# A transformer decoder layer on Trainium2: residuals added by TensorE, LayerNorm sums formed by ScalarE

## Chip, cores and metric

The kernel runs on 1 core of one Trainium2 chip. The metric is the device time of one execution in microseconds (us), the median of 3 runs.

## What is computed

Batch 8, sequence 512, width 512, 16 heads of 32. Three blocks, each followed by a residual sum and a LayerNorm for the first two, and once more for the MLP:

```python
x1 = layernorm(x  + self_attention(x))                 # rope, softmax over 512 keys, no output projection
x2 = layernorm(x1 + tree_attention(x1, ctx) @ Wo.T + bo)
y  = layernorm(x2 + relu(x2 @ w1 + b1) @ w2 + b2)      # width 2048
```

`tree_attention` builds keys and values from `ctx`, adds a binary tree of sums above them (1023 nodes), and lets every position attend to itself and to 12 nodes that an index table names.

## The kernel before

All large products are made in fp16 in three parts: an fp32 operand is split into `hi` and `lo`, and `hi*hi + hi*lo + lo*hi` is accumulated in fp32. Engines run their own instruction streams and meet only through semaphores; the order on each engine is written out by hand.

The first stage walks over the batch. `iteration` has 32 steps `d` (a head pair and a quarter of the keys each): scores and row maxima (`rows_ps`, `neg_max`, VectorE), exponentials (`e_ps` to `probsT`, ScalarE) and values (`o_ps`) with a lag of 12 to 14 steps, and beside them the projections of the next batch (`AUX_AT`), the tree (`tree`, GpSimd) and the splitting of later weights. LayerNorm of the batch before lies in steps 15 to 19 (`LN_STEPS`): `add_residual` on GpSimd, `norm_stats` and `norm_apply` on VectorE, `rstd_of` on GpSimd. At step 19 SyncE (SP) stores the four tiles of x1 in fp32 to `x1_dram` (L365), from which the second stage reads them. A last `iteration(..., tail=True)` finishes the last batch; then all engines meet at the border of the stages.

The second stage works on tiles of 128 positions (4 per batch, 32 in all); two tiles are a round. VectorE and GpSimd do tree attention for round r+1 while TensorE and ScalarE do the MLP of round r.
- VectorE, `attention`, per tile: `key_sums` for the groups 2 to 5 of gathered rows and the own row (L1358, L1362, L1367), `shift` (L1385 to L1391), `x2_sum` of the tile before (L1451 residual, L1454 and L1457 statistics), `key_sums` for groups 0 and 1 of the next tile, `normalise` (L1397 to L1404), `values` (L1416, L1420, L1426; accumulated in PSUM tile `O`). In each second tile `y_sums` (L1466, L1469) for the round before lies behind the first accumulation.
- GpSimd, `attention`, per tile: `x2_rstd_of`, the value products of groups 3, 4 and 5 (`weight_values`), 12 gathers of 128 rows of 4 KB (L1533), each after the slot that it fills was accumulated, then `y_adds` (L1595) or `y_rstds`. There are 8 slots for groups of two gathers.
- TensorE and ScalarE, `mlp`, per round: 16 chunks `c` of 128 hidden columns. TensorE: `hidden(c)` (12 products), then the attention products that are due, then `mlp_out(c-1)` (6 products), then `hidden_minus_hi(c)`. ScalarE: `hid_hi(c)` (L1288), its attention work, `hid_lo(c)` (L1311). `OUT_AT`, `QUERY_AT`, `EXP_AT`, `APPLY_AT`, `X2_AT` say at which chunk the attention work of the two tiles lies: `copy_o` (L1248) and the output projection, the query projection, the exponentials (L1252), the x2 normalisation (L1259), the x2 transpose.
- A transposed tile is split in turns: TensorE transposes into `TURN`, ScalarE copies `hi` (L1233), TensorE subtracts it (`turn_minus_hi`), ScalarE copies `lo` (L1235).
- `PROJ` and `O` are one PSUM bank. `copy_acc` copies the MLP's result at the start of the next round (L1274), `y_apply` normalises it at the end of that round (L1266).

Middle rounds run in hardware loops of two rounds (one loop pass is four tiles).

## Time and profile before

| | |
|---|---|
| runs (us) | 2434.88, 2438.08, 2434.06; median 2434.88 |
| profiled execution | 2434.74 us, its span 2432.9 us |
| TensorE busy | 2066.2 us (85%) |
| VectorE busy | 1701.0 us (70%) |
| GpSimd busy | 1050.4 us (43%) |
| ScalarE busy | 985.0 us (40%) |
| granted TensorE clock, mean | 0.937 |

The span runs from the first to the last instruction. In the rows, DVE is VectorE, ACT is ScalarE, POOL is GpSimd, PE is TensorE, SPq is the queue of SyncE that issues DMAs. A timeline row is start (us), duration (us), engine, line, operation, output<-input, shape, count, and in brackets the idle time before it and what ended that. A group row has the count, then busy us, mean ns of one, then idle us before them. Matmuls are pipelined, and their ends are modelled.

### The profile page before, as it was taken

Reading aid. Unit: us, or ns where it says so; the run is one execution under the profiler, and the core shown is the slowest. Engines: PE = TensorE matmul, PEld = TensorE weight load, DVE = VectorE, ACT = ScalarE, POOL = GpSimd, SP = SyncE. Lnnn points to the kernel's source line nnn. Section 1 sums busy time; section 2 is a strip of 40 time slices with the busy share of each in tenths; the row PEclk is TensorE's granted clock in tenths of the full one; section 3 lists DMA queues with packets and bytes.
Section 4 is the critical chain, followed back from the end, with each engine's and each line's share of the span. In section 5 each row is a group of like instructions: output and inputs, shape, how many; then the busy total and the mean of one; then the engine's idle time right before and its main releaser. Section 6 shows DMA issues by size and latency. Waiting matters only on the chain.

```text
span 2432.9 us, 33921 instructions
## 1 busy us (share of the span) xinstructions
PE 2066.2 (85%) x10944; PEld 1014.4 (42%) x10944; DVE 1701.0 (70%) x2289; ACT 985.0 (40%) x1579; POOL 1050.4 (43%) x1132
## 2 busy tenths in 40 slices
PE   5899999999999999994239888898888898888987
PEld 2333333333333333331015554455554555545554
DVE  8565647475565647552788888898888988988950
ACT  3355445454545455553013333333333333333333
POOL 3232334242433424233354655655656546556521
PEclk9999999999999999997669999999999999999999
DMA  6442424343343424233945656556556556566510
GB/s 206 133 135 91 131 84 147 106 139 118 118 148 117 139 76 145 88 126 119 361 165 202 229 173 222 202 189 227 191 202 232 180 201 225 185 220 215 177 63 27
DMA packets 189290, 392.50 MB, mean 161 GB/s; under 512 B 20948, under 2 KB 82516, under 8 KB 189144
## 3 DMA queue, kind: packets, MB, share of 16 engines
q1 hardware_dynamic: 133848, 189.44, 24.4%
q0 software_dynamic: 55296, 201.35, 23.6%
q8 instruction: 63, 1.03, 0.2%
q14 instruction: 83, 0.68, 0.1%
HBM read 312.86 MB, written 77.59 MB: 160 GB/s over the span
## 4 chain that ended last, share of the span: by engine, by line
DVE 25%; issue 11%; DMA 8%; PE 5%; POOL 3%; SPq 1%; DVEq 0%; ACT 0%; POOLq 0%
DVE bank L1420 8%; DMA nb<-kv_flat,idx_rows 7%; DVE logits L1367 4%; DVE nb L1416 4%; POOL nb L1533 2%; PE bank L1136 2%; DVE nb L1358 2%; PE bank L1117 2%; DMA own<-kv_flat 1%; DVE stats L1454 1%; DVE x L1451 1%; DVE own L1362 1%; DVE bank L1426 1%; DVE stats L1466 1%; PE bank L1084 1%
## 5 line engine op out<-in xcount | busy, mean ns | idle before, releaser
L697 DVE TENSOR_REDUCE neg_max<-rows_ps 128x2 f32<-128x1024 f32 x256 | 312.5, 1221 | 309.0 <-PE rows_ps L492 308.1
L1533 POOL DMA_INDIRECT nb<-kv_flat,idx_rows x384 | 367.6, 957 | 136.0 <-issue 85.0
L1358 DVE TENSOR_TENSOR nb<-nb,bank 128x1024 f32<-128x1024 f32 x192 | 230.6, 1218 | 137.1 <-DMA nb<-kv_flat,idx_rows 108.6
L617 ACT ACTIVATE probsT<-e_ps 128x1024 f32<-128x1024 f32 x256 | 262.0, 1023 | 158.4 <-PE e_ps L520 158.1
L1117 PE MATMUL bank<-x2T_hi,w_hi_sb 128*128 128x256 f16 x1024 | 285.9, 279 | 5.6 <-issue 4.8
L1117 PE MATMUL bank<-x2T_lo,w_hi_sb 128*128 128x256 f16 x1024 | 285.2, 279 | 0.0
L1117 PE MATMUL bank<-x2T_hi,w_lo_sb 128*128 128x256 f16 x1024 | 284.5, 278 | 0.0
L510 PE MATMUL o_ps<-probsT,v_sb 128*33 128x512 f32 x1024 | 272.9, 612 | 6.3 <-ACT oT L614 6.1
L1420 DVE TENSOR_TENSOR bank<-bank,nb 128x512 f32<-128x512 f32 x384 | 268.1, 698 | 13.7
L1561 POOL TENSOR_TENSOR nb<-nb,weights 128x1024 f32<-128x1024 f32 x96 | 182.7, 1917 | 155.6 <-DVE weights L1404 154.9
L1367 DVE TENSOR_REDUCE logits<-nb 128x32 f32<-128x1024 f32 x192 | 229.9, 1211 | 0.0
L443 PE MATMUL aux<-in_hi,w_hi 128*128 128x512 f16 x512 | 196.8, 384 | 38.0 <-DVE w_lo L653 28.1
L1136 PE MATMUL bank<-w_hi_sb,hid_hi 128*128 128x512 f16 x512 | 203.9, 398 | 19.9 <-ACT hid_lo L1311 19.9
L1136 PE MATMUL bank<-w_hi_sb,hid_lo 128*128 128x512 f16 x512 | 204.9, 400 | 0.0
L1136 PE MATMUL bank<-w_lo_sb,hid_hi 128*128 128x512 f16 x512 | 204.8, 400 | 0.0
L765 POOL TENSOR_TENSOR lo<-rot,hi 128x512 f16<-128x512 f32 x64 | 78.0, 1219 | 290.8 <-DVE hi L676 290.8
L1311 ACT ACTIVATE hid_lo<-bank,b_sb 128x256 f16<-128x256 f32 x256 | 120.5, 471 | 194.0 <-PE bank L1124 194.0
L443 PE MATMUL aux<-in_hi,w_lo 128*128 128x512 f16 x512 | 196.7, 384 | 0.0
L443 PE MATMUL aux<-in_lo,w_hi 128*128 128x512 f16 x512 | 196.6, 384 | 0.0
L492 PE MATMUL rows_ps<-k_stack,q_stack 96*128 96x512 f16 x512 | 153.8, 381 | 37.6 <-DVE neg_max L697 37.4
L1288 ACT ACTIVATE hid_hi<-bank,b_down 128x256 f16<-128x256 f32 x256 | 121.1, 473 | 155.0 <-PE bank L1117 154.1
L760 POOL TENSOR_TENSOR in_lo<-in_sb,in_hi 128x2048 f16<-128x2048 f32 x16 | 68.7, 4295 | 226.1 <-ACT in_hi L554 226.1
(147 smaller groups left out, 3583.2 us busy)
## 6 DMA issues: line engine op xcount, KB each, us to landing
kv_flat<-kv_nat SPq DMA_DIRECT2D x128, 256.0 KB, 3.4
own<-kv_flat SPq DMA_DIRECT2D x32, 512.0 KB
q_stack<-qk_dram SPq DMA_DIRECT2D x96, 128.0 KB, 2.9
k_stack<-qk_dram SPq DMA_DIRECT2D x96, 128.0 KB, 3.2
piece<-in_pieces SPq DMA_DIRECT2D x40, 256.0 KB, 3.0
in_sb<-in_xT SPq DMA_DIRECT2D x8, 1024.0 KB, 6.5
in_sb<-in_ctxT SPq DMA_DIRECT2D x8, 1024.0 KB, 5.8
qk_dram<-hi SPq DMA_DIRECT2D x32, 256.0 KB, 2.2
```

The lines of the kernel that those rows point to most:

```text
L443: mm = pe.matmul(o[:], w_part[:, w, c, f], x_part[:, which, c, :], start=c + k == 0, stop=c == KC - 1 and k == 2)
L492: mm = pe.matmul(rows_ps[:, i, :], q_stack[0:M_ROW, h, qt * P:(qt + 1) * P], k_stack[0:M_ROW, h, :], start=True, stop=True)
L510: mm = pe.matmul(O[side * SIDE:side * SIDE + VW, :], v_sb[:, slot, kt, 2 * pair + side, :], probsT[:, (d - V_LAG) % TT, side, :], start=kt ...
L617: act.activation(probsT[:, (d - E_LAG) % TT, :, :], e_ps[:], ACT.Exp, scale=1.0 / (Q_UP * K_UP))\
L697: dve.tensor_reduce(neg_max[:, g % 2, at:at + 2], rows_ps[:], AX.X, ALU.max, negate=True).then_inc(max_done, 1)
L1117: mm = pe.matmul(HB[c % 2][:, 0:RW], w[:, k, c * P:(c + 1) * P], x_part[:, k, half * RW:(half + 1) * RW], start=k + i == 0, stop=k == KC - ...
L1136: mm = pe.matmul(ACC[i][:], h_part[:, c % 2, i * P:(i + 1) * P], w[:, c, :], start=False, stop=c == WC - 1 and k == 2)
L1358: dve.tensor_tensor(kk, kk, q.unsqueeze(1).to_broadcast([P, GN, D]), ALU.mult)\
L1367: dve.tensor_reduce(logits[:, lt % 2, g * GN:(g + 1) * GN, :], nb[:, slot(lt, g), :, 0:D].rearrange("p n (h d) -> p n h d", h=H), AX.X, AL ...
L1420: dve.tensor_tensor(O[:], O[:], nb[:, slot(lt, g), k, D:2 * D], ALU.add).then_inc(o_part, 1)
L1533: pool.indirect_dma_start(nb[:, slot(lt, g), k, :], None, kv_flat, bass.IndirectOffsetOnAxis(idx_rows[:, lt, at:at + 1], 0))\
L1561: pool.tensor_tensor(vv, vv, w, ALU.mult).then_inc(v_mul_pool, 1)
```

## The change

In the first stage, x1 is split after LayerNorm: ScalarE copies each tile to fp16 (`x1_parts` hi), GpSimd subtracts (lo); this lies in steps 18, 19 and 22, the stores of two tiles each in steps 20 and 24, and the tail has 25 steps in place of 20. The query's rope tables are those of the key, and the query's scale is put into the copy from PSUM.

In the second stage x1 comes in as two fp16 parts. The query needs no split: 8 fp16 transposes into one bank and one copy. `project_out` adds x1 by two products with `plus_up` (64 times the identity), `mlp_out(0)` adds x2 by 8 products of 128 columns for each tile. ScalarE copies PROJ and ACC with an accumulated sum (`x2_sum`, `copy_acc`), then forms the sum of squares about the mean with `Square` (`x2_square`, `y_square`). VectorE's `x2_sum` and `y_sums` and GpSimd's `y_adds` are gone. `x2_rstd_of` moves from the head of the next tile's GpSimd work to the end of the tile's own. `OUT_AT`, `EXP_AT` and the first `QUERY_AT` and second one move by one chunk; `y_apply` moves to chunk 7 of the round.

```diff
-TAIL = 20
+TAIL = 25
-X1_STORE, X_ROWS_LOAD, X_ROWS_BIAS = 19, 21, 27
+X1_SPLIT = {18: (0,), 19: (1,), 22: (2, 3)}
+X1_STORE, X_ROWS_LOAD, X_ROWS_BIAS = (20, 24), 24, 27
-OUT_AT, QUERY_AT, EXP_AT, APPLY_AT, X2_AT = (1, 9), (2, 8), (4, 12), (5, 13), (6, 14)
+OUT_AT, QUERY_AT, EXP_AT, X2_AT = (2, 10), (3, 9), (5, 13), (6, 14)
+SUM_AT, SQUARE_AT, APPLY_AT = (3, 11), (4, 12), (5, 13)
+Y_SQUARE_AT, Y_APPLY_AT = 1, 7
...
# first stage: load_x waits for the split, not the store; two stores
-                    sp.wait_ge(x1_stored, START + b * (16 * TT))
+                    sp.wait_ge(x1_lo_done, START + b * TT)
+                def store_x1(b, k):
+                    sp.wait_ge(x1_lo_done, START + b * TT + 2 * k + 2)
...
# first stage, ScalarE
+                            for t in X1_SPLIT.get(d, ()):
+                                act.wait_ge(x1_ready, START + (b - 1) * TT + t + 1)
+                                act.wait_ge(x1_stored, START + (b - 1) * 32 + 16 * (t // 2))
+                                act.activation(x1_parts[:, t % 2, 0, :], xb[:, t, :], ACT.Copy).then_inc(x1_hi_done, 1)
# first stage, GpSimd
+                            for t in X1_SPLIT.get(d, ()):
+                                pool.wait_ge(x1_hi_done, START + (b - 1) * TT + t + 1)
+                                pool.tensor_tensor(x1_parts[:, t % 2, 1, :], xb[:, t, :], x1_parts[:, t % 2, 0, :],
+                                                   ALU.subtract).then_inc(x1_lo_done, 1)
...
# second stage, SyncE
                 def load_res(b, lt):
-                    sp.wait_ge(out_added, START + b * TT + lt)
+                    sp.wait_ge(proj_ready, START + b * TT + lt)
# second stage, TensorE
                 def turn_query(b, lt):
-                    turn(turn_of(b, lt, "q"), x1_in[:, lt % 2, :])
+                    pe.wait_ge(turn_copied, START + turn_of(b, lt, "q"))
+                    for k in range(2):
+                        for f in range(KC):
+                            at = (k * KC + f) * P
+                            mm = pe.transpose(TURN16[:, at:at + P], x1_in[:, lt % 2, k, f * P:(f + 1) * P], plus_one[:])
+                    mm.then_inc(turn_ready, 1)
                 def project_out(b, lt):
-                    pe.wait_ge(out_added, START + b * TT + lt)
+                    pe.wait_ge(res_loaded, START + (b * TT + lt) * 16 + 16)
+                    for k in range(2):
+                        pe.matmul(PROJ[:], plus_up[:], x1_res[:, k, :], start=False, stop=False)
# mlp_out, c == 0
+                            for k in range(KC):
+                                for x_part in (x2T_hi, x2T_lo):
+                                    pe.matmul(ACC[i][:, k * P:(k + 1) * P], x_part[:, k, rows], plus_up[:],
+                                              start=False, stop=False)
...
# second stage, ScalarE
+                def turned_query(b, lt):
+                    act.wait_ge(turn_ready, START + turn_of(b, lt, "q") + 1)
+                    act.activation(actT[:, ACT_SLOT["q", lt % RT]].rearrange("p k c t -> p (k c t)"), TURN16, ACT.Copy)\
+                        .then_inc(turn_copied, 1)
+                def x2_sum(b, lt):
+                    act.wait_ge(proj_ready, START + n + 1)
+                    act.activation(x2[:, s, :], PROJ[:], ACT.Copy, scale=1.0 / W_UP, accum_out=sums[:, s:s + 1])\
+                        .then_inc(x2_summed, 1)
+                    act.wait_ge(x2_summed, START + n + 1)
+                    act.activation(neg_mean[:, s:s + 1], sums[:, s:s + 1], ACT.Copy, scale=-1.0 / D)\
+                        .then_inc(x2_centre, 1)
+                def x2_square(b, lt):
+                    act.wait_ge(x2_centre, START + n + 1)
+                    act.wait_ge(x2_squared, START + n)
+                    act.activation(squares[:, 0, :], x2[:, s, :], ACT.Square, bias=neg_mean[:, s:s + 1],
+                                   accum_out=sum_squares[:, s:s + 1]).then_inc(x2_squared, 1)
# copy_acc: the same accum_out; y_square(b, half) squares both tiles of a round at chunk 1
...
# second stage, VectorE
-                    dve.scalar_tensor_tensor(out=x2[:, lt, :], in0=PROJ[:], scalar=1.0 / W_UP, in1=x1_res[:],
-                                             op0=ALU.mult, op1=ALU.add).then_inc(out_added, 1)
-                    dve.bn_stats(stats[:, s, :], x2[:, lt, :]).then_inc(x2_part, 1)
-                    dve.bn_aggr(mean_var[:, s, :], stats[:, s, :]).then_inc(x2_stats, 1)
-                        dve.bn_stats(stats[:, s, :], y_sb[:, lt, :]).then_inc(y_part, 1)
-                        dve.bn_aggr(mean_var[:, s, :], stats[:, s, :]).then_inc(y_stats, 1)
# values
-                        dve.wait_ge(o_copied, START + n)
+                        dve.wait_ge(x2_summed, START + n)
# second stage, GpSimd, attention
-                        if not (early and lt == 0):
-                            x2_rstd_of(*last_tile(b, lt))
...
-                            y_adds(b - 1, half_)
-                        if lt % RT == 1 and not early:
                             y_rstds(b - 1, half_)
+                        x2_rstd_of(b, lt)
```

## Rows read from the trace of the kernel before

**Rows 1.** Busy time by stage: us, then PE, PEld, DVE, ACT, POOL, clock, DMA share, GB/s

```profile
60.00:1050.00 990.00, 932.17 (x4365) 362.69 (x4364) 586.63 (x826) 490.49 (x643) 340.32 (x351) 0.99 0.39 120
...
1300.00:2347.00 1047.00, 904.53 (x5456) 544.22 (x5454) 904.23 (x1188) 377.87 (x760) 582.51 (x641) 0.93 0.58 201
```

**Rows 2.** Timeline of VectorE: the weights of tiles 4 and 30

```profile
1337.25 0.37 DVE L1404 TENSOR_TENSOR weights<-weights,total 128x208 f32<-128x208 f32 x1
...
2301.15 0.37 DVE L1404 TENSOR_TENSOR weights<-weights,total 128x208 f32<-128x208 f32 x1
```

**Rows 3.** Timeline of VectorE over one tile, from weights to weights

```profile
1782.95 0.37 DVE L1404 TENSOR_TENSOR weights<-weights,total 128x208 f32<-128x208 f32 x1
...
1805.93 1.22 DVE L1358 TENSOR_TENSOR nb<-nb,bank 128x1024 f32<-128x1024 f32 x1 [0.95 <-DMA nb<-kv_flat,idx_rows]
...
1811.86 0.69 DVE L1451 SCALAR_TENSOR_TENSOR x<-bank,x_res 128x512 f32<-128x512 f32 x1
...
1813.61 2.35 DVE L1358 TENSOR_TENSOR nb<-nb,bank 128x1024 f32<-128x1024 f32 x2
...
1818.14 0.50 DVE L1397 TENSOR_REDUCE total<-weights 128x16 f32<-128x208 f32 x1
...
1819.25 0.37 DVE L1404 TENSOR_TENSOR weights<-weights,total 128x208 f32<-128x208 f32 x1
```

**Rows 4.** Timeline of GpSimd in that tile: first and eighth gather

```profile
1788.34 1.05 POOL L1533 DMA_INDIRECT nb<-kv_flat,idx_rows  x1 [1.06 <-DVE bank L1420]
...
1799.02 0.94 POOL L1533 DMA_INDIRECT nb<-kv_flat,idx_rows  x1 [0.30 <-issue]
```

**Rows 5.** Timeline of VectorE in the next tile, the last of a loop pass

```profile
1823.73 0.68 DVE L1466 BATCH_NORM_STATS2 stats<-y_sb 128x6 f32<-128x512 f32 x1
...
1825.62 0.70 DVE L1420 TENSOR_TENSOR bank<-bank,nb 128x512 f32<-128x512 f32 x1
...
1838.88 2.35 DVE L1358 TENSOR_TENSOR nb<-nb,bank 128x1024 f32<-128x1024 f32 x2 [4.96 <-issue]
...
1857.92 0.37 DVE L1404 TENSOR_TENSOR weights<-weights,total 128x208 f32<-128x208 f32 x1
```

**Rows 6.** Timeline of ScalarE in these tiles

```profile
1795.88 0.60 ACT L1248 ACTIVATE o_sb<-bank 128x512 f32<-128x512 f32 x1 [6.42 <-DVE bank L1420]
...
1815.34 0.37 ACT L1252 ACTIVATE weights<-logits 128x208 f32<-128x208 f32 x1
...
1850.58 0.38 ACT L1252 ACTIVATE weights<-logits 128x208 f32<-128x208 f32 x1 [1.75 <-DVE logits L1391]
```

**Rows 7.** Busy time after two waits for `copy_o`, columns as in rows 1

```profile
1685.00:1691.00 6.00, 5.41 (x33) 3.19 (x34) 1.34 (x2) 2.94 (x6) 4.71 (x5) 1.00 0.99 353
1796.00:1802.00 6.00, 5.40 (x17) 2.07 (x18) 3.11 (x3) 1.57 (x4) 4.48 (x6) 0.54 0.85 330
```

**Rows 8.** Groups of ScalarE, and one product of TensorE from its timeline

```profile
L1259 ACT ACTIVATE x<-x,shift_by,rstd 128x512 f32<-128x512 f32 x32 | 25.8, 807 | 28.6 <-POOL shift_by L1573 28.6
L617 ACT ACTIVATE probsT<-e_ps 128x1024 f32<-128x1024 f32 x256 | 262.0, 1023 | 158.4 <-PE e_ps L520 158.1
1815.20 0.38 PE L1136 MATMUL bank<-w_hi_sb,hid_lo 128*128 128x512 f16 x1
```

**Rows 9.** First stage, timelines of VectorE and GpSimd, and a GpSimd group

```profile
941.90 3.39 DVE L689 TENSOR_SCALAR xb<-xb,mean_var,rstd 128x512 f32<-128x512 f32 x2
941.93 5.87 POOL L775 TENSOR_TENSOR kvT<-kvT 128x1024 f32<-128x1024 f32 x9
L765 POOL TENSOR_TENSOR lo<-rot,hi 128x512 f16<-128x512 f32 x8 | 9.3, 1157 | 38.7 <-DVE hi L676 38.7
```

**Rows 10.** Border of the stages: timelines of GpSimd and ScalarE, and the x1 stores' landing

```profile
1129.98 0.56 POOL L791 TENSOR_TENSOR rstd<-var_eps,half 128x1 f32<-128x1 f32 x1
1133.81 0.31 ACT L1220 ACTIVATE minus_one<-ident 128x128 f16<-128x128 f32 x1 [14.67 <-PEq L210]
DMA to landing us min/median/max: 2.0/2.0/2.3
```

More of the change, by code:

```diff
@@ L57 @@
 Q_UP, K_UP = 64.0, 16.0
+Q_MORE = SCALE * Q_UP / K_UP
 W_UP = 64.0
@@ L1273, in copy_acc, with y_square, y_apply @@
                     for lt in tiles(half):
-                        act.activation(y_sb[:, lt, :], ACC[lt % RT][:], ACT.Copy, scale=1.0 / W_UP)\
-                            .then_inc(acc_copied, 1)
+                        s = 2 + lt % 2
+                        act.activation(y_sb[:, lt, :], ACC[lt % RT][:], ACT.Copy, scale=1.0 / W_UP,
+                                       accum_out=sums[:, s:s + 1]).then_inc(acc_copied, 1)
+                    act.wait_ge(acc_copied, START + (b * 2 + half + 1) * RT)
+                    act.activation(neg_mean[:, 2:4], sums[:, 2:4], ACT.Copy, scale=-1.0 / D).then_inc(y_centre, 1)
+                def y_square(b, half):
+                    act.wait_ge(y_centre, START + b * 2 + half + 1)
+                    act.wait_ge(y_squared, START + (b * 2 + half) * RT)
+                    for lt in tiles(half):
+                        s = 2 + lt % 2
+                        act.activation(squares[:, 1 + lt % RT, :], y_sb[:, lt, :], ACT.Square, bias=neg_mean[:, s:s + 1],
+                                       accum_out=sum_squares[:, s:s + 1]).then_inc(y_squared, 1)
+                def y_apply(b, half):
+                    act.wait_ge(y_rstd, START + b * 2 + half + 1)
+                    for lt in tiles(half):
+                        s = 2 + lt % 2
+                        act.activation(y_sb[:, lt, :], y_sb[:, lt, :], ACT.Identity, scale=rstd[:, s:s + 1],
+                                       bias=shift_by[:, s:s + 1]).then_inc(y_ready, 1)
                 def mlp(b, half, attend, more):
@@ L1300, in mlp @@
                         if more and c == QUERY_AT[1]:
-                            turned(qb, qh * RT + 1, "q")
+                            turned_query(qb, qh * RT + 1)
                         if attend and c == OUT_AT[1]:
-                            turned(ab, second, "o")
+                            turned_out(ab, second)
                         if more and c == EXP_AT[1]:
                             exponentials(qb, qh * RT)
+                        if attend and c == SUM_AT[1]:
+                            x2_sum(ab, second)
+                        if attend and c == SQUARE_AT[1]:
+                            x2_square(ab, second)
                         if attend and c == APPLY_AT[1]:
                             x2_apply(ab, second)
+                        if after_first and c == Y_SQUARE_AT:
+                            y_square(*last_round(b, half))
+                        if after_first and c == Y_APPLY_AT:
+                            y_apply(*last_round(b, half))
                         if attend and c == X2_AT[1]:
@@ L1316, in mlp @@
                             copy_o(ab, second)
[L1317 to L1318 removed]
                 for lt in range(RT):
[L1321 removed]
+                    turned_query(0, lt)
                 exponentials(0, 0)
                 copy_o(0, 0)
[L1324 to L1325 removed]
+                turned_out(0, 0)
+                x2_sum(0, 0)
+                turned_query(0, RT)
+                x2_square(0, 0)
                 exponentials(0, 1)
@@ L1482, in attention @@
                         normalise(b, lt)
-                        def between():
-                            if lt % RT == 1 and not (isinstance(b, int) and b == 0):
-                                y_sums(b - 1, half)
-                        values(b, lt, between)
+                        values(b, lt)
                 dve.memset(ones_rows[:], 1.0).then_inc(bias_step, 1)
@@ L1515, in _ @@
                 attention(B - 1, 1, False)
-                x2_sum(B - 1, TT - 1)
-                y_sums(B - 1, 0)
-                y_sums(B - 1, 1)
             @block.gpsimd
@@ L1629, in _ @@
                 attention(B - 1, 1, False)
-                x2_rstd_of(B - 1, TT - 1)
                 for half_ in range(2):
-                    y_adds(B - 1, half_)
                     y_rstds(B - 1, half_)
```

203 lines of the change are left out of this document (87 added, 116 removed).

## The prediction, made before the changed kernel was run

> **What bounds the kernel now.** I read first the busy time by stage, then the timelines of VectorE, GpSimd and ScalarE over one tile of the second stage, then the border between the stages. The first stage (self-attention, until about 1131 us) is TensorE's: it is busy 932 of 990 us, VectorE 587, ScalarE 490 [rows 1]. The second (cross-attention and MLP) has TensorE at 905 of 1047 us, VectorE at 904, ScalarE at 378, and DMA at a mean share of 0.58. No engine is full there, so the order of waits decides. One tile is one pass of `attention`; 26 tiles take 2301.15 - 1337.25 = 963.9 us, 37.07 each [rows 2].
>
> The cycle closes through the gathers. VectorE has the weights at 1782.95; GpSimd starts the first gather at 1788.34 and the one that holds group 5 of the next tile at 1799.02 [rows 3, 4]. GpSimd's issue, 1.25 us a gather (957 ns and a gap), fills that stretch. VectorE waits for the data until 1805.93, then works without a wait: the last products, `shift`, at 1811.86 `x2_sum`, at 1813.61 the next tile's first keys, at 1818.14 `normalise`, at 1819.25 the next weights. That is 36.3 us, in which TensorE, ScalarE's copies and the y sums have no part. TensorE follows: ScalarE waits 6.42 us for VectorE's last accumulation before `copy_o` of a first tile [rows 6]. So work taken off VectorE between the gather wait and the weights counts in full; work taken off elsewhere doesn't, until the cover ends.
>
> **The change part by part.**
>
> (a) `x2_sum` leaves VectorE: 1813.61 - 1811.86 = 1.75 us a tile, on the chain [rows 3]. It stands ahead of the weights of tiles 1 to 31: 31 x 1.75 = 54.3 us. The next limit is the same chain, shorter: GpSimd's last gather of the tile is the fourth after 1799.02, so it ends by 1805, long before the next weights.
>
> (b) `y_sums` leaves VectorE: 1825.62 - 1823.73 = 1.89 us in each second tile [rows 5]. It stands after the accumulation of group 0, while GpSimd is still issuing, and VectorE then waits for the landing of group 5 anyway [rows 3]: worth nothing there. The exception is the tile at the hardware loop's branch: VectorE stands 4.96 us, and no gather is late after that. Weights to weights is 38.67 us (1857.92 - 1819.25); without (a) and (b) it is 35.0, and the gather chain asks 36.3 - 1.75 = 34.6. So (b) gives up to 1.89 more; I take 1.7, in 6 loop passes: 10.2 us. Ends: 0 and 11.3.
>
> (c) GpSimd's `y_adds` (two tensor additions a round) end its queue, behind the last gather: 0.
>
> (d) ScalarE gains, per tile, the x2 copy with a sum (0.60, taking the place of nothing), the tiny mean, the square and the y square (0.80 each, by the activation with pointer operands [rows 8]), and four accumulator results, which no row here shows: between 0 and 0.37 each (the 128x208 activation in rows 6); I take 0.2. The query's two copies of 0.60 become one of 1024 elements: 1.02. Sum about 3.3 us a tile on an engine busy 378 of 1047 us. Each insert sits between `hid_hi` and `hid_lo`, where TensorE has the previous chunk's six products and the next hidden product to do; a chunk is at most 4.0 us (32 us of TensorE a tile, by its busy share of 905 in 1047, over 8 chunks), and I estimate the cover at 1.5 of them; `y_square` (2 us) overruns it by half a microsecond. TensorE had 6.42 us idle in front of `copy_o`, so this is worth 0 as long as that idle lasts.
>
> (e) TensorE gains, per round, 4 products for x1 (at most 0.38 each [rows 8]; matmuls overlap, so I take 0.2), 16 of 128 columns for x2 (a quarter of the columns of that row: 0.08), and 16 fp16 transposes for 8 fp32 ones, and loses two `minus_hi`. About +2 us in a round of 74; at 0.38 for each of the 28 additional ones it would be 10.6. TensorE's idle time is (1047 - 905) / 1047 x 74 = 10 us a round, so even the upper end is nearly covered: 0.
>
> (f) `OUT_AT`, `EXP_AT` move one chunk later with `copy_o`, so the distance from `copy_o` to `exponentials` holds: 1815.34 - 1795.88 = 19.46 us. VectorE wants the result at 1818.14, that is 22.26 after `copy_o`; without `x2_sum` at 20.5. The exponentials take 0.37, so 0.7 us of margin is left in a first tile. Two things move it: about +0.4 us for two x1 products and, the other way, the clock. After the 6.42 us wait TensorE was granted 0.54 of its clock (near the 1.2 GHz level); in the stretch after a 3.2 us wait 1.00 (2.4 GHz) [rows 7]. The waits get shorter by (a), (d) and (e), to some 2 to 3 us, so I expect the full clock and an earlier exponential. In second tiles ScalarE waits 1.75 us for VectorE at this point, so there is more room. Taken: 1 us lost in all. Ends: -0 and +16 x 1.5 = 24 us.
>
> (g) GpSimd's `x2_rstd_of` now ends a tile's queue and waits for ScalarE's square. Behind it stands the next tile's `weight_values`, then the gathers, so this is a dangerous wait. The square is one chunk before the exponentials' place, at about `copy_o` + 15, and three tiny operations take 1.3 us: `copy_o` + 16.5 = 29.5 us after the weights, against 34.6 for the next. Covered by 5 us. SP's loads of x1 wait for `proj_ready`, some 10 us after `copy_o`, earlier than for VectorE's sum; `load_own` behind them waits for a later event. VectorE's first write to `O` now waits for `x2_summed`, over 10 us early. All 0.
>
> (h) The end: `copy_o` of the last tile comes after one more chunk, so one chunk less follows it (some 3 us, at most 4.0); the added products, sums and `y_square` on the open path give about as much back. Taken 0, ends -3 and +3.
>
> (i) First stage, steady part. ScalarE gets 4 copies of 0.60 a batch, GpSimd 4 subtractions of 1.16. The copies come behind an exponential of 1.02, and ScalarE is idle half of this stage [rows 1, 8]: 0 for them. GpSimd's are the more dangerous: while its tree additions run from 941.93, two `norm_apply` of VectorE take 3.39 us together [rows 9], where other VectorE operations on 128x512 take 0.7 [rows 3], and the row maximum behind them comes late for TensorE. The new subtractions push the tree back; what they block on VectorE partly replaces what the tree blocks. I take +0.7 us a batch, 7 batches: +5. Ends: -1 a batch (the tree no longer hits `norm_apply`), -7, and everything in series, 4 x (0.60 + 1.16) = 7 a batch, +49.
> The Trainium skill, GPSIMD Engine Reference, Key points, says that GpSimd shares its SBUF interfaces with VectorE and contends with VectorE instructions that read two SBUF inputs or use a two-port mode. The 3.39 us row agrees. By this rule alone the subtractions cost VectorE 4 x 1.16 = 4.6 us a batch, 32 in all, if each met such an instruction.
>
> (j) The stage border. Before, the last rstd is done at 1130.5, x1 stores land in 2.0 us, and the second stage starts at 1133.81 [rows 10]. Now behind GpSimd's last rstd (1129.98 + 0.56) come two subtractions of 1.16 (to 1132.9), a store (2.0, and 0.3 to issue by my estimate, to 1135.2), because `x1_parts` holds two tiles, ScalarE's next copy (0.60, to 1135.8), two more subtractions (to 1138.1) and the second store (to 1140.4). The old one had landed about 0.3 us ahead of 1133.81: +6.9 us, and +8 with the semaphores between five engines' steps. Nothing covers this. Ends +5 and +10.
>
> Sum: -54.3 - 10.2 + 1 + 0 + 5 + 8 = -50.5. The profiled execution took 2434.74 us (span 2432.9 and 1.8 around it), the median of the runs is 2434.88; so 2384.
>
> **The rivals.**
> R1, the first stage pays (i): ScalarE and GpSimd additions expose themselves between steps 18 and 24. For it: VectorE is already held up there. Against: TensorE's idle time of this stage is 58 us in all [rows 1]. At the upper end, 49 in place of 5: 2434.7 - 50.5 + 44 = 2428; half of it 2406.
> R2, slower: the exponentials come late. Place: `exponentials(ab, second)`, behind the query copy, sum and square. If the 2.9 us of these, the 0.8 of x1 products and an accumulator cost at its upper end stand in series, it comes 4 us later; VectorE waits 4 - 0.7 = 3.3 us in 16 first tiles and some 1.5 in 15 second ones: 53 + 22 = 75 us, 2434.7 - 50.5 + 75 = 2459. It decides the sign from about 3.9 us of delay in first tiles alone (16 x 3.2 = 51). Against: these inserts have TensorE's six products and a projection beside them. 1 us later instead costs 16 x 0.3 = 5; 2 us, 21: 2405.
> R3, the gathers don't follow: the DMA share in the bursts is already 0.85 to 0.99 [rows 7], so a shorter tile only moves waiting to `nb`. If half of (a) is lost: 2384 + 27 = 2411. If all: 2384 + 54 = 2438. For it: the wait before 1805.93. Against: the burst of 12 gathers ends 14 us before the next weights, and the mean share is 0.58.
>
> **How the numbers follow.** My forecast (chain shorter by 1.75 a tile, small losses) 0.60; its own range is 2370 to 2398. R1 0.12, mild R2 or R3 (2400 to 2415) 0.16, R3 in full about 0.03 (no change or slightly slower), R2 in full 0.05, something better still (earlier waits, full clock) 0.04. Range for 8 in 10: 2364 to 2414. A difference below 0.2% (5 us) is about what a measurement of this kernel can't tell from none. Faster 0.91, same 0.03, slower 0.06.
>
> **What would show it.** Weights to weights at 35.3 us on average, 35 at the loop's branch; no `x2_sum` or `y_sums` rows on VectorE, the wait for gathers before the fourth key product still there; ScalarE's wait before `copy_o` down to 2 to 3 us with the clock at 1.00 behind it; the exponentials done before VectorE reaches `normalise`; the second stage starting 13 us later than 1133.8. The forecast is wrong if VectorE shows waits for ScalarE's weights, if GpSimd's weight products start later than 0.2 us after the weights (a late `x2_rstd_of`), or if a batch in the first stage is over 2 us longer.

## The result, and the profile after

The changed kernel took 2364.25 us (median of 4 runs, 2362.97 to 2364.82), the kernel before 2435.34 in the same measurement (median of 4): ratio 0.9705, 95% interval 0.9689 to 0.972. Ratios and their intervals, here and below, leave out slow executions, over 1.5% above the kernel's fastest; medians in us are of all executions. The profiled execution took 2364.57 us, its span is 2362.4, 70.5 less than before. The forecast was 2384, so 20 us of the gain were not foreseen. The tiles of the second stage gave less than the sum had for them, the first stage and the end gave more.

| stretch | before | after | difference | in the sum |
|---|---|---|---|---|
| first stage, to the start of its last TensorE products | 1119.28 | 1101.67 | -17.6 | +5 |
| border, to the second stage's first ScalarE work | 14.53 | 23.07 | +8.5 | +8 |
| from there to the weights of tile 0 | 44.67 | 46.04 | +1.4 | 0 |
| weights of tile 0 to weights of tile 31 | 1154.13 | 1097.17 | -57.0 | -64.5 and +1 |
| weights of tile 31 to the end of the span | 100.29 | 94.45 | -5.8 | 0 |

The weights' timeline rows, the kernel after, answer to [rows 2]: 26 tiles take 916.25 us, 35.24 each, where they took 37.07.

```profile
1321.25 0.37 DVE L1481 TENSOR_TENSOR weights<-weights,total 128x208 f32<-128x208 f32 x1
...
2237.50 0.37 DVE L1481 TENSOR_TENSOR weights<-weights,total 128x208 f32<-128x208 f32 x1
```

VectorE in the tile that answers to [rows 3], the kernel after:

```profile
1744.84 0.37 DVE L1481 TENSOR_TENSOR weights<-weights,total 128x208 f32<-128x208 f32 x1
...
1768.87 1.22 DVE L1435 TENSOR_TENSOR nb<-nb,bank 128x1024 f32<-128x1024 f32 x1 [1.24 <-DMA nb<-kv_flat,idx_rows]
...
1774.50 0.38 DVE L1468 TENSOR_TENSOR logits<-logits,top 128x208 f32<-128x208 f32 x1
1774.79 1.21 DVE L1435 TENSOR_TENSOR nb<-nb,bank 128x1024 f32<-128x1024 f32 x1
1776.36 1.22 DVE L1435 TENSOR_TENSOR nb<-nb,bank 128x1024 f32<-128x1024 f32 x1 [0.35 <-DMA nb<-kv_flat,idx_rows]
...
1780.86 0.37 DVE L1481 TENSOR_TENSOR weights<-weights,total 128x208 f32<-128x208 f32 x1
```

Behind `shift` (1774.50) the next tile's keys follow at once: `x2_sum` is gone. The wait of 0.35 us between the two key products is new; in [rows 3] both ran as one pair without a gap. The second product starts 31.5 us after the weights (1776.36 - 1744.84), when its rows are there; before, it started some 31.8 us after them, behind `x2_sum`, and so met no wait.

**Where the first stage gained.** VectorE's row maxima (`neg_max`, 256 of them) are clocks for this stage. Until the 50th both traces agree within 0.3 us. Then all of the gain comes in jumps, each within steps 20 to 25 of a batch: 3.4, 1.9, 3.4, 1.8, 3.3, 1.7 and 2.2 us. The first six lie in batches 1 to 6. The last lies in batch 7, which has no `in_lo`; b_two_subs and b_two_stores below, which gain nothing in the six, jump by 2.5 and 1.6 us there as well. So 15.5 of the 17.6 us belong to the encounter shown here. The first jump, the kernel before, timelines of VectorE, GpSimd and TensorE:

```profile
275.30 4.45 DVE L673 TENSOR_TENSOR rot<-rot,shuf 128x512 f32<-128x512 f32 x1
...
280.25 1.22 DVE L697 TENSOR_REDUCE neg_max<-rows_ps 128x2 f32<-128x1024 f32 x1
...
266.87 5.87 POOL L775 TENSOR_TENSOR kvT<-kvT 128x1024 f32<-128x1024 f32 x9
274.68 4.52 POOL L760 TENSOR_TENSOR in_lo<-in_sb,in_hi 128x2048 f16<-128x2048 f32 x1 [1.94 <-ACT in_hi L554]
...
281.52 0.60 PE L492 MATMUL rows_ps<-k_stack,q_stack 96*128 96x512 f16 x2 [2.84 <-DVE neg_max L697]
```

and the kernel after:

```profile
275.43 0.69 DVE L688 TENSOR_TENSOR rot<-rot,shuf 128x512 f32<-128x512 f32 x1
276.28 0.47 DVE L691 CAST hi<-rot 128x512 f16<-128x512 f32 x1 [0.15 <-DVE rot L688]
276.67 1.21 DVE L712 TENSOR_REDUCE neg_max<-rows_ps 128x2 f32<-128x1024 f32 x1
...
266.95 2.45 POOL L821 TENSOR_TENSOR x_parts<-xb,x_parts 128x512 f16<-128x512 f32 x2
269.37 7.10 POOL L790 TENSOR_TENSOR kvT<-kvT 128x1024 f32<-128x1024 f32 x9
276.41 4.27 POOL L775 TENSOR_TENSOR in_lo<-in_sb,in_hi 128x2048 f16<-128x2048 f32 x1
```

Before, GpSimd began `in_lo` at 274.68. The last step of VectorE's rotation (275.30), 0.69 us of work, stood until `in_lo` was done; the row maximum behind it came 3.6 us late, and TensorE waited 2.84 us. Why every second jump is the smaller one (1.7 to 1.9) was not followed up. After, the two subtractions of x1 push the tree back by 2.5 us and `in_lo`, which had waited 1.94 us for its input before, by 1.73; the rotation and its cast begin ahead of `in_lo`, by 0.13 us.

**The border**, the kernel after, timelines of GpSimd, SP's queue and ScalarE, answers to [rows 10]:

```profile
1112.90 2.45 POOL L821 TENSOR_TENSOR x_parts<-xb,x_parts 128x512 f16<-128x512 f32 x2
...
1115.43 6.35 SPq L371 DMA_DIRECT2D x_dram<-x_parts  x2
...
1118.33 1.15 ACT L633 ACTIVATE x_parts<-xb 128x512 f16<-128x512 f32 x2 [6.86 <-DMA x_dram<-x_parts]
...
1119.04 2.26 POOL L821 TENSOR_TENSOR x_parts<-xb,x_parts 128x512 f16<-128x512 f32 x2 [3.70 <-ACT x_parts L633]
...
1124.74 0.31 ACT L1249 ACTIVATE minus_one<-ident 128x128 f16<-128x128 f32 x1 [5.26 <-PEq L214]
```

The chain is the one that the prediction wrote down: subtract, store, wait for the landing (ScalarE, 6.86 us), copy, subtract, store.

### The profile page after: what moved, and what is told of

Same layout as the page of the kernel before. It is cut to its first block, busy times and chain, and to the rows that moved or that the text cites. A ratio compares the mean times of both kernels' runs of the same rounds, so it can differ in the third digit from the quotient of the medians.

```text
span 2362.4 us, 34653 instructions
## 1 busy us (share of the span) xinstructions
PE 2045.6 (87%) x11360; PEld 1021.0 (43%) x11360; DVE 1617.2 (68%) x2129; ACT 1071.9 (45%) x1854; POOL 1037.1 (44%) x1084
## 3 DMA queue, kind: packets, MB, share of 16 engines
q8 instruction: 108, 1.77, 0.3%
## 4 chain that ended last, share of the span: by engine, by line
DVE 21%; DMA 12%; issue 9%; POOL 5%; PE 4%; SPq 1%; ACT 0%; DVEq 0%; POOLq 0%; ACTq 0%
DMA nb<-kv_flat,idx_rows 10%; DVE bank L1497 9%; POOL nb L1568 5%; DVE nb L1493 5%; DVE logits L1444 3%; PE bank L1172 2%; PE bank L1148 1%; DVE nb L1435 1%; DMA own<-kv_flat 1%; DVE bank L1503 1%; DVE total L1474 1%; SPq L1067 1%; DVE weights L1481 0%; DVE own L1439 0%; PE bank L1108 0%
## 5 line engine op out<-in xcount | busy, mean ns | idle before, releaser
L1172 PE MATMUL bank<-w_hi_sb,hid_hi 128*128 128x512 f16 x512 | 198.7, 388 | 9.1 <-ACT hid_lo L1386 9.1
L1172 PE MATMUL bank<-w_hi_sb,hid_lo 128*128 128x512 f16 x512 | 199.1, 389 | 0.0
L1172 PE MATMUL bank<-w_lo_sb,hid_hi 128*128 128x512 f16 x512 | 198.8, 388 | 0.0
```

What stands on the lines that cost most here:

```text
L1172: mm = pe.matmul(ACC[i][:], h_part[:, c % 2, i * P:(i + 1) * P], w[:, c, :], start=False, stop=c == WC - 1 and k == 2)
```

## The experiments

The later measurements ran in other sessions, on three chips. There the kernel before took 2434 to 2447 us (on one chip 2446 and 2436 in two sessions, on another 2446 and 2434, so the chip alone does not set it), and the changed kernel did not take 2364, as a run of it will show. So a run is compared with what ran beside it, and, where only one stretch matters, by the clock of that stretch: the last row maximum of the first stage, relative to the kernel before, and the periods from weights to weights.

### The first stage: place or queue

One edit each, on the kernel before (the first three) and on the changed kernel (the fourth):

```diff
# b_two_subs: GpSimd, behind the rstds of steps 18 and 19
+ pool.tensor_tensor(more_lo[:], bv_sb[:], bv_sb[:], ALU.subtract)
# b_in_lo_later: GpSimd, in_lo from step 20 to behind the low part of step 21
-                        if d == CTX_SPLIT and not last:
-                            split(1, 3 + 2 * b)
                         for kind, i in aux_items(d - 1, first, last):
                             if kind == "qk":
                                 low_part((b + 1) * 2 * KC + i, i)
+                                if d == CTX_SPLIT + 1:
+                                    split(1, 3 + 2 * b)
# b_two_stores: SyncE
-X1_STORE, X_ROWS_LOAD, X_ROWS_BIAS = 19, 21, 27
+X1_STORE, X_ROWS_LOAD, X_ROWS_BIAS = (20, 24), 24, 27
# (and the tail of 25 steps, stores of two tiles each)
# a_splits_late
-X1_SPLIT = {18: (0,), 19: (1,), 22: (2, 3)}
+X1_SPLIT = {21: (0, 1), 22: (2, 3)}
-X1_STORE, X_ROWS_LOAD, X_ROWS_BIAS = (20, 24), 24, 27
+X1_STORE, X_ROWS_LOAD, X_ROWS_BIAS = (22, 24), 24, 27
```

> The kernel before with nothing but two more subtractions on GpSimd in each batch of the first stage, in steps 18 and 19 ahead of the tree additions (a constant minus itself, 128x512, into a scratch tile that nobody reads); no copy on ScalarE, no other store. Theory P (place): the gain of the first stage comes from the subtraction of in_lo (4.5 us) starting some 1.7 us later, so that it no longer holds VectorE's rotation (4.45 us in place of 0.69) in front of a row maximum. Then added work makes the first stage 15 to 19 us shorter: about 2418 us in all. Theory Q (queue): the gain comes from SyncE, which no longer issues four stores of x1 in step 19. Then nothing is gained: 2435 to 2440 us.

Measured: 2447.2 us beside 2446.2 for the kernel before, ratio 1.0001 (0.9977 to 1.0025). The first stage is 0.9 us shorter. A miss of the expected 17, and a telling one. Timelines of VectorE and GpSimd:

```profile
275.48 4.21 DVE L678 CAST hi<-rot 128x512 f16<-128x512 f32 x1 [0.15 <-DVE rot L675]
...
266.18 2.22 POOL L808 TENSOR_TENSOR more_lo<-bv_sb 128x512 f16<-128x512 f32 x2
268.36 7.03 POOL L777 TENSOR_TENSOR kvT<-kvT 128x1024 f32<-128x1024 f32 x9
275.34 4.06 POOL L762 TENSOR_TENSOR in_lo<-in_sb,in_hi 128x2048 f16<-128x2048 f32 x1
```

Here `in_lo` (275.34) begins 0.14 us before the cast of the rotation (275.48), and the cast of 0.43 us takes 4.21. In the changed kernel it began 0.13 us behind the cast. Whichever of the two starts first runs, and the other stands until its end: the 3 us hang on some 0.3 us.

> The kernel before with one order changed: GpSimd makes in_lo behind the low part of the rotation in step 21, in place of step 20. No work is added or taken away. Theory P: the rotation no longer meets it, and it ends before the next rotation begins, so at least as much as in the change: 17 to 25 us less, 2410 to 2418 us. Theory Q: no change, 2435 us.

Measured: 2417.9 us beside 2446.2, ratio 0.9885 (0.9851 to 0.9919). The first stage is 28.0 us shorter than before, more than the 17 to 25 expected, and batch 0, in which the change does nothing, gives 3.3 of it. All 56 instructions of the line that stood for 4.45 us take 691 to 694 ns now. Reordering `in_lo` alone is worth more than the change's by-product.

> The kernel before with SyncE's part of the first stage as in the change: x1 (still fp32, from xb) in two stores of two tiles, in steps 20 and 24, the load of the next x in step 24. GpSimd, VectorE and ScalarE are as before. Theory P: nothing, 2433 to 2437 us. Theory Q: the 17 us, 2418 us.

Measured: 2445.8 us, ratio 0.9994 (0.9974 to 1.0014), first stage +0.6 us. SyncE's queue has no part in it.

> The changed kernel with the splits of x1 moved from steps 18, 19 and 22 to 21 and 22, the first store to step 22: the same work, but nothing more stands ahead of the tree and of in_lo on GpSimd. Theory P: in_lo starts at its old place and meets the rotation again; the first stage gives its 17 us back: about 2381 us, more if the four subtractions meet a rotation as well. Theory Q: 2362 to 2367 us, as SyncE's work is still that of the change.

Measured: 2476.2 us; first stage 17.3 us longer than before, 34.9 longer than in the changed kernel, twice what was expected. `in_lo` begins at 275.73, the rotation at 276.35 stands 4.46 us, and the subtractions now lie on its cast (1.14 us for 0.43) and on the second rotation as well; how much of the 34.9 is theirs was not separated. (Its total also holds the stalls of the next section.)

### Stalls that the first measurement did not have

The next four runs came out 31 to 101 us above what was expected of them, so they were followed by the changed kernel itself.

```diff
# a_in_lo_later: the edit of b_in_lo_later on the changed kernel
# a_in_lo_24: the same, and
-X1_SPLIT = {18: (0,), 19: (1,), 22: (2, 3)}
+X1_SPLIT = {18: (0,), 19: (1,), 24: (2, 3)}
-X1_STORE, X_ROWS_LOAD, X_ROWS_BIAS = (20, 24), 24, 27
+X1_STORE, X_ROWS_LOAD, X_ROWS_BIAS = (20, 25), 25, 27
# a_dve_x2, in attention of VectorE behind shift(b, lt): operations on a scratch tile `more`
+ dve.scalar_tensor_tensor(out=more[:, 0, :], in0=more[:, 1, :], scalar=1.0 / W_UP, in1=more[:, 1, :], ...)
+ dve.bn_stats(...); dve.bn_aggr(...)
# a_dve_y, in values behind group 0 of each second tile
+ twice: dve.bn_stats(...); dve.bn_aggr(...)
```

> The changed kernel with the order of the earlier experiment: GpSimd makes in_lo behind the low part of the rotation (step 21). Theory P (a VectorE operation on SBUF that starts while in_lo runs stands until it ends): in batch 0, which has no splits to push in_lo back, the stall of 3.3 us goes; in batches 1 to 6 in_lo, now some 1.5 us later than in the change (277.9 to 282.2 in batch 1), meets the first product of the second rotation (281.15), which costs up to 1 us and is partly hidden: 0 to +1 a batch. Sum -3.3 to +3 us: 2361 to 2367 us. If the gain were only a matter of what stands ahead on GpSimd's queue: no change in batch 0 either.

Measured: 2435.5 us. First stage: 19.2 us shorter than before, 3.6 more than the changed kernel when it ran next (a_again: 15.6), most of it in batch 0, as Theory P has it. The total is 70 us above the expected.

> As the run before it, and the last two splits of x1 moved from step 22 to 24 (second store and the load of x in step 25), so that no subtraction stands beside the second rotation (1.2, 1.64 and 1.53 us for its three products in the change, 0.7 alone). Theory P: batch 0 gives 3.3, each of batches 1 to 6 another 1 to 2 us: 10 to 15 us less than the changed kernel, about 2352 us. If GpSimd's subtractions of x1 cost VectorE nothing that TensorE sees: 2361 us.

Measured: 2453.0 us, first stage only 7.7 us shorter than before: worse, not better. In batch 1 the gain up to step 25 is 1.5 us larger than in the run above, as expected; behind it 4.1 us are lost again, in step 30 (in batches 2 to 5, 5.1 to 1.8 us in the same step). Its trace puts that on the moved transfers and not on the subtractions. The load of the next x is issued at 289.67, where the run above has it at 281.92, and now goes out right ahead of the next input's load and the stores of keys and values. ScalarE waits for one of these stores to land (the run above has no such wait), TensorE for ScalarE's copy, and the row maximum 3.87 us for TensorE:

```profile
300.59 1.09 ACT L606 ACTIVATE kv_nat<-aux 128x512 f32<-128x512 f32 x2 [2.38 <-DMA kv_flat<-kv_nat]
301.24 0.61 PE L457 MATMUL aux<-w_hi,in_hi 128*128 128x512 f16 x1 [2.78 <-ACT kv_nat L606]
```

No run moves the transfers alone, so this is read from the trace only.

> The changed kernel with 1.75 us of VectorE work back at the place of x2_sum, on scratch tiles (one scalar_tensor_tensor, bn_stats and bn_aggr on 128x512 behind shift, in tiles 1 to 31); nothing waits for it. The prediction's term (a), in full on the chain: +54 us, 2418 us. Theory G (the gathers take a part): without x2_sum VectorE stands 0.35 to 0.5 us for the rows of the next tile's group 1, which that work had hidden, so it costs only 1.25 to 1.4 a tile: +39 to +44 us, about 2406 us.

> The changed kernel with 1.9 us of VectorE work back at the place of y_sums, on scratch tiles (bn_stats and bn_aggr twice, behind the first accumulated group of each second tile from the third round on); nothing waits for it. The prediction's term (b): nothing in a tile that waits for its gathers behind it, 1.7 us in the six at the hardware loop's branch: +10 us, 2374 us. Rival: it counts in full in all 14 places, as VectorE's later accumulations are what frees the slots: +27 us, 2391 us. Other rival: 0, as the branch stall has room too.

Measured: 2448.9 and 2462.0 us. With the stalls in them these totals tell nothing about the two terms; both were made again further down.

> The changed kernel itself, with nothing altered, as the standard for the last four runs, which all lost 70 to 90 us in the second stage, of which 7 to 12 us in each tile behind the hardware loop's branch, where ScalarE and TensorE stood for instructions. Theory S (surroundings): how long the fetch of instructions behind the branch takes under the burst of gathers differs between chips or sessions and has nothing to do with the edits; then this run is as slow: 2430 to 2445 us, and in it the tiles 7, 11, 15, 19, 23 and 27 take 46 us. Theory E (edit): the edits caused it; then this run takes 2364 us, with 35 to 36 us for these tiles.

Measured: 2425.5 us (2419.3 to 2430.6) beside 2435.8 for the kernel before, ratio 0.9944 (0.9918 to 0.9971). Theory S holds: the changed kernel is itself 61 us slower here. Periods: 46.6 us (median) for the tiles 7, 11, ..., 27, where the first measurement had 35.9, and 34.0 to 35.7 in the other places of the loop. In one such tile, timelines of ScalarE and VectorE:

```profile
1415.07 0.47 ACT L1386 ACTIVATE hid_lo<-bank,b_sb 128x256 f16<-128x256 f32 x1 [8.26 <-remote]
1415.44 0.59 ACT L1283 ACTIVATE o_sb<-bank 128x512 f32<-128x512 f32 x1
...
1425.67 1.02 ACT L1269 ACTIVATE actT<-bank 128x1024 f16<-128x1024 f16 x1 [3.42 <-PE bank L1123]
...
1431.09 2.35 DVE L1435 TENSOR_TENSOR nb<-nb,bank 128x1024 f32<-128x1024 f32 x2 [10.83 <-PE bank L1108]
```

ScalarE stands 8.26 us, and what ended that is no instruction that the profile has ("remote"; "issue" means that it shows nothing at all that was waited for); `copy_o`, the query's copy (1425.67) and the query's projection come late, and VectorE stands 10.83 us for the query of the next tile. From 1180 to 2300 us ScalarE's "remote" and "issue" waits sum to 235.5 us; in the first measurement's traces, before and after, they are 0.

### Without the branch

```diff
# a_unrolled (and b_unrolled on the kernel before), second stage
-                with pe.Fori(0, B - 1) as b:
+                for b in range(0, B - 1):
-                with act.Fori(0, B - 2) as b:
+                for b in range(0, B - 2):
# a_unrolled_in_lo: both edits (a_unrolled, a_in_lo_later);  u_dve_x2, u_dve_y, u_out_early: those of the a_ names on a_unrolled
# a_out_early (and u_out_early)
-OUT_AT, QUERY_AT, EXP_AT, X2_AT = (2, 10), (3, 9), (5, 13), (6, 14)
-SUM_AT, SQUARE_AT, APPLY_AT = (3, 11), (4, 12), (5, 13)
+OUT_AT, QUERY_AT, EXP_AT, X2_AT = (1, 9), (2, 8), (4, 12), (6, 14)
+SUM_AT, SQUARE_AT, APPLY_AT = (2, 10), (3, 11), (5, 13)
```

> The changed kernel itself once more, as the standard beside the next two. Theory S (surroundings): 2364 us or 2420 to 2430 us, depending on the chip; in the second case the whole difference is in the tiles 7, 11, 15, 19, 23 and 27.

> The changed kernel with TensorE's and ScalarE's loops of the second stage written out (the same instructions in a straight line, no branch; VectorE, GpSimd and SyncE keep their loops). Theory F (fetch behind the branch): the two engines stand for instructions because a taken branch asks for a new page of the program while the gathers hold the DMA engines; without a branch the tiles 7, 11, ... take 35 to 36 us, and the run 2360 to 2368 us on any chip. Rival: the fetch is slow wherever a new page begins; a longer straight program needs more pages, and the stalls are spread over all tiles: 2425 us or more.

> The run before it and GpSimd's in_lo behind the low part of the rotation in step 21. Under both theories 1 to 5 us less than the run before it, all of it in the first stage (batch 0 gives 3.3 us): 2357 to 2365 us by Theory F.

> The kernel before with TensorE's and ScalarE's loops of the second stage written out. It had few of these stalls (37 us for the tiles where the changed kernel took 46), so by Theory F it gains little: 0 to 10 us, 2435 us; the change is then worth 2435 - 2370 = 65 us or so once no engine stands for instructions. Rival: writing the loops out is worth some 60 us in any kernel; then 2380 us, and the change is worth next to nothing.

Measured, the first three side by side: 2440.7 for the changed kernel (ratio to the kernel before 0.9981, 0.9955 to 1.0007), 2377.8 with the loops written out (0.9743, 0.9666 to 0.9821; four runs, 2370 to 2401), 2367.2 with `in_lo` moved as well (0.9659, 0.9611 to 0.9708; six runs, 2360 to 2397). Of the 10.6 us between these two the first stage gives 4.8, within the 1 to 5 expected; the rest is no more than their runs spread. In a_again2 the tiles 7, 11, ..., 27 take 46.0 us (median), as in a_again. The kernel before with its loops written out: 2431.7 beside 2434.1, ratio 0.9988 (0.9972 to 1.0005). So writing the loops out is worth 63 us to the changed kernel by the medians (58 by the ratios), and to the one before nothing that can be told from none.

The time came near what Theory F said (2377.8 for 2360 to 2368), the reason did not hold. ScalarE's "remote" and "issue" waits, 1180 to 2300 us, against VectorE's waits for a query's projection:

| kernel | ScalarE's | VectorE's for the query |
|---|---|---|
| before and after, first measurement | 0 | 0.5 and 0.4 |
| before with in_lo moved (b_in_lo_later) | 200 | 5 |
| after (a_again) | 235 | 71 |
| after, loops written out (a_unrolled) | 237 | 17 |
| the same, one chunk earlier (u_out_early) | 237 | 65 |

The stalls stay when the branch goes; they fall at other places of the round. Where such a stall lies between the round's start and the query's copy, VectorE's next keys wait for it; elsewhere TensorE's and ScalarE's slack takes it. In u_out_early each of the 12 tiles in which VectorE waits over 1.5 us for the query has a stall of 7.2 to 9.2 us ahead of the query's copy; a_unrolled has such waits in two tiles. ScalarE at two places of a_unrolled, one without cost and one with 5.11 us ahead of the query (that tile took 42 us):

```profile
1629.94 0.47 ACT L1351 ACTIVATE hid_hi<-bank,b_down 128x256 f16<-128x256 f32 x1 [7.39 <-remote]
...
1699.57 0.60 ACT L1265 ACTIVATE actT<-bank 128x512 f16<-128x512 f32 x1 [5.11 <-remote]
```

### The two terms again, and the end

> a_unrolled with the 1.75 us of VectorE work back at the place of x2_sum in tiles 1 to 31. In full on the chain (the prediction's (a)): +54 us over a_unrolled, 2425 to 2432 us. Theory G (the gathers take part of it, as the waits for rows grow when this work goes): +39 to +44 us, 2412 to 2420 us.

> a_unrolled with the 1.9 us of VectorE work back at the place of y_sums. The prediction's (b): +10 us in all (1.7 in six tiles, behind VectorE's own loop branch), 2380 to 2390 us. If it counted in each of the 14 places: +27 us, 2397 to 2405 us.

Measured on one chip, side by side: 2413.5 and 2364.25 us. a_unrolled itself did not run beside them (2377.8 us is from a session in which the kernel before took 12 us more), so the totals are not set against it. Weights of tile 0 to weights of tile 31: 1146.4 us with the x2 work, 1097.2 with the y work, and 1097.2 in the first trace of the changed kernel without either. That the last two agree to a tenth is chance, as the run with the y work holds 9.9 us of waits for the query. But place by place it is no longer than a_unrolled (medians 35.17, 35.01, 35.46 and 33.96 us in the order of those below): the y work costs nothing that can be seen. The x2 work costs 49.2 us, not 54.3: 1.2 to 1.3 us a tile in three places of the loop and 2.45 in the tile at VectorE's loop branch (medians 37.05, 36.34, 36.87 and 36.87 us against 35.75, 35.13, 35.60 and 34.42 in a_unrolled), which makes some 48 us over 31 tiles, an estimate that needs no other session's total. That is Theory G's figure for the ordinary tile, and more than the work itself at the branch. There VectorE stands again as in [rows 5], u_dve_x2:

```profile
1676.57 2.35 DVE L1438 TENSOR_TENSOR nb<-nb,bank 128x1024 f32<-128x1024 f32 x2 [5.33 <-issue]
```

In the kernel before this wait is 4.5 to 5.1 us in five of these tiles, in the changed kernel it is gone and a wait for gathered rows of 3.4 to 4.7 us stands in the tile. Why the x2 work brings it back is open.

> The changed kernel with copy_o, the query's turn, the x2 sum, its square and the exponentials one chunk earlier, where the kernel before had them (APPLY_AT and X2_AT stay). VectorE's chain from weights to weights is not touched. The prediction's step (h): the end, from the last tile's weights, is one chunk longer, 2.7 us, and more if TensorE's wait in front of copy_o brings the clock down again (some 2 us): +3 to +5 us there. In the steady tiles nothing: periods within 0.3 us of those of the changed kernel run beside it. Rival: the longer wait of ScalarE and TensorE in front of copy_o lowers the clock in each tile and makes the exponentials late: +1 us in each first tile, 20 us in all.

> a_unrolled with copy_o and what hangs on it one chunk earlier (as in a_out_early). The end, from the last tile's weights to the last copy of ACC, was 87.1 us before and 82.8 after; with the chunk back it is 2.7 us longer, and 4 to 5 us if TensorE's wait in front of copy_o takes the clock down again. In the steady tiles nothing (35.2 us as before). Rival: every tile gets longer, because the wait comes earlier in the round and TensorE runs on a lower clock behind it: +1 us a tile, 30 us.

Measured: 2454.3 us for the first, and 2426.8 for the second. From the last weights to the span's end both take 97.1 us, a_unrolled 94.4: 2.7, one chunk. The clock stays at 1.00 behind its last `copy_o`, so that part of the expectation fails. The tiles did get longer, by the stall of the table above, brought back ahead of the query: from the first weights to the last u_out_early takes 48.4 us more than a_unrolled, and its waits for the query are 47.7 us longer. The clock behind `copy_o` of the first tiles is lower as well (0.50 to 0.72 in most, where a_unrolled has 1.00 in nearly all), as the rival said; what it adds to these waits was not separated.

## Why the prediction was right or wrong, step by step

(a) `x2_sum`: the mechanism is right, the size was 49.2 for 54.3. In the ordinary tile about 0.5 of the 1.75 us turns into waits for gathered rows (0.35 us at 1776.36): the mild form of R3, which had been priced against the sum and not put into it. VectorE's waits for rows from 1180 to 2330 us grew from 106.5 to 145.9 us; 23.9 of that took the place of its waits at the loop's branch, and the 15.5 left are 0.5 a tile.

(b) `y_sums`: nothing speaks against its counting only at VectorE's loop branch. That tile lost 3.64 us (38.24 to 34.60, medians), forecast 3.65, and the match is luck: the x2 work is worth 2.45 of it in place of 1.75, which leaves 1.2 for the y work in place of 1.89. u_dve_y shows that once `x2_sum` is away the y work costs nothing even there: VectorE's waits for rows in that tile are 3.7 us in a_unrolled and 1.7 with the y work (medians). Together (a) and (b) gave 57.0 of 64.5, so 7.8 are left for (b) where it had 10.2. The 35.3 us a tile that the prediction named as its sign, and that 35.24 meets, leaves (b) out; by its sum it should have been 35.0.

(c), (d), (e), (g): nothing in the trace speaks against the zeros, and no run tested them alone. `x2_rstd_of` is done at 1771.2, ten microseconds ahead of the weights at 1780.86, and GpSimd's products start 0.54 us behind the start of the weights, as before.

(f) In the first measurement the exponentials hold VectorE once, for 0.81 us ahead of the last tile's weights (2266.83); for 17 of the 32 ScalarE waits for VectorE's logits. With the later sessions' stalls they do come late, 12.2 us in all in a_again2: R2's wait by another cause. The forecast for ScalarE's wait in front of `copy_o` held for every other tile only. It is 2.99 us in one, 5.93 in the next and 0 in the one after, and the clock behind the second is 0.72, where [rows 7] had 0.54:

```profile
1757.77 0.60 ACT L1283 ACTIVATE o_sb<-bank 128x512 f32<-128x512 f32 x1 [2.99 <-DVE bank L1497]
...
1793.79 0.60 ACT L1283 ACTIVATE o_sb<-bank 128x512 f32<-128x512 f32 x1 [5.93 <-DVE bank L1497]
```

(h) The end: forecast 0, measured -5.8. One chunk less is 2.7 (u_out_early). What was set against it wasn't there: from the first of the last two copies of ACC on the end took 11.70 us in place of 13.21, as squares on ScalarE are a shorter way than sums through GpSimd and VectorE. The remaining 1.6 us go with the wait in front of the last `copy_o` (3.83 before, 1.86 after) and the clock behind it, 0.72 and 1.00; this part is argued.

(i) The first stage is the step that failed: +5 forecast, -17.6 measured, and outside both ends that were given (-7 and +49). The prediction read that GpSimd holds up VectorE, and looked at one place, the tree against `norm_apply` [rows 9]. It asked what the new subtractions would run into, not what they would push away. The costly encounter of this stage was another: `in_lo` against the rotation, 4.45 us where 0.69 is the norm, and the row maximum behind it. b_in_lo_later removes it by order alone and gets 28 us; b_two_subs puts as many subtractions in front of `in_lo` as the change and, 0.27 us off, gets nothing: that the change got its 15.5 us was a matter of tenths of a microsecond, not of design.
The Trainium skill, SBUF — State Buffer, section "SBUF: two separate sides", has the rule for this: the pair of ports that GpSimd and VectorE share is an exclusive lock between a GpSimd operation and a VectorE operation that has two SBUF inputs or runs in a two-port mode, and whichever starts first keeps it for its whole instruction. The traces agree: the rotation ends 0.55 us behind `in_lo`, and 0.14 us decide in b_two_subs. The prediction had priced the new instructions by overlap; with a lock, the order of starts decides.

(j) The border: +8 forecast, +8.5 measured, by the steps as written. The +1.4 us between it and the first weights lie within what other runs show there (44.4 to 46.6 us).

In the first measurement R1 and R2 did not come true, R3 in small. Outside the forecast altogether lay the query. The change moves its copy and projection a chunk later (`QUERY_AT`), and in the first measurement nothing waited for it (0.4 us in all). Where ScalarE's stalls fall ahead of it, most of the 61 to 76 us of the later sessions hangs on it (65 to 71 us of waits); that the kernel before, with the query earlier, loses only 5 to 11 us to it is shown, that `QUERY_AT` is the reason is argued. VectorE's own work is a rival: with the x2 work back, `QUERY_AT` unchanged, the wait is 33 us in a_dve_x2 where a_again has 71, and 0 in u_dve_x2. u_out_early speaks against it in its simple form, since it has the query early again and still waits: what counts is where the stall lies, and that shifts with every instruction added.

## What to carry to other kernels

Work added to GpSimd is not only priced by what it blocks: list every long GpSimd instruction behind it and the VectorE instruction that each of them meets, and ask which pairs change their order. An instruction that takes six times its usual time in a timeline (4.45 us where the rest of its group takes 0.69) is worth more than its own row suggests, and moving one line may remove it.
When one engine's work leaves the path, read the next two limits off the same rows: here the gathers took 0.5 us a tile at once, and in the sessions in which ScalarE stalled the query was next.
Run the changed kernel again in another session before trusting a gain: the same file gave 2.95% in one and 0.2 to 0.6% in two others.

## What the runs showed of the hardware

- A gain of 3 us a batch hung on which of two instructions started 0.14 us earlier (GpSimd's `in_lo`, VectorE's cast).
- In the later sessions, on three chips, ScalarE stood 153 to 255 us of 1120 without another engine as the cause, with every kernel; in the first measurement 0. Of the two instruction queues one moved 108 packets, 1.77 MB (16.4 KB each), in every trace of the changed kernel, the other 60 or 61 of 8 KB, and when ScalarE stood at 1407 to 1415 the DMA engines were full with gathers (share 1.01). In the first measurement they were as full in that stretch (0.99), and ScalarE did not stand, so a full share alone is not enough. That it waited for its program is argued from this, not shown.
  The Trainium skill, Runtime: NRT & Kernel Launch, section "Instruction fetch mechanics", says that the program streams in blocks of 16 KiB and that a taken branch to outside the two blocks held forces a fetch before the engine goes on. The packets of the one queue agree, those of the other do not; the second part would explain the place in a_again, but the waits did not shrink when the branches went (235 and 237 us).
- Writing TensorE's and ScalarE's loops out was worth some 60 us to one kernel and nothing measurable to the other, and with `in_lo` moved gave the lowest ratio of all to the kernel before, 0.9659, though its interval (0.9611 to 0.9708) takes in the 0.9705 of the first measurement.
